# Reciprocals of linear attention spread to the heads' rows by DMA instead of by matmul

## What is computed

```python
qp = _phi(proj(Wq, bq))          # elu(x) + 1
kp = _phi(proj(Wk, bk))
v = proj(Wv, bv)
def step(carry, inp):
    kv, ksum = carry
    kt, vt, qt = inp
    kv = kv + jnp.einsum('bhd,bhe->bhde', kt, vt)
    ksum = ksum + kt
    num = jnp.einsum('bhd,bhde->bhe', qt, kv)
    den = jnp.einsum('bhd,bhd->bh', qt, ksum)[..., None] + EPS
    return ((kv, ksum), num / den)
```

## Time and profile before

| | us |
|---|---|
| median of three runs | 1916.9 (1913.78 to 1916.97) |
| profiled execution | 1916.06 |
| its span | 1914.3 |
| PE busy | 1890.7 |
| DVE busy | 1569.2 |
| POOL busy | 889.8 |
| ACT busy | 663.8 |

### The profile page before, as it was taken

How to read it: one execution, slowest core, us unless ns; L and a number is a source line. 1 busy time by engine, 2 the same in 40 slices (tenths; PEclk the granted TensorE clock), 3 DMA queues, 4 the chain that set the end, 5 groups by cost and what they waited for, 6 DMA issues and landing times.

```text
span 1914.3 us, 60181 instructions
## 1 busy us (share of the span) xinstructions
PE 1890.7 (99%) x25412; PEld 1659.6 (87%) x25412; DVE 1569.2 (82%) x3356; ACT 663.8 (35%) x1298; POOL 889.8 (46%) x981
## 2 busy tenths in 40 slices
PE   7999999999999999999999999999999999999997
PEld 6888888888888888888888888888888888888887
DVE  7888787888879888778878888887888897888888
ACT  4333333323333332333333433333333333323331
POOL 4345554455443554534554445544345553455422
PEclk9999999999999999999999999999999999999999
DMA  6343234333243432343323334333443234333222
GB/s 215 101 128 112 96 106 128 118 118 112 90 127 119 127 121 74 123 125 116 123 89 118 117 112 136 100 98 113 128 128 112 85 114 130 117 117 113 89 73 90
DMA packets 171197, 217.97 MB, mean 114 GB/s; under 512 B 24368, under 2 KB 85808, under 8 KB 170928
## 3 DMA queue, kind: packets, MB, share of 16 engines
q1 hardware_dynamic: 170928, 214.13, 35.4%
HBM read 151.02 MB, written 63.04 MB: 112 GB/s over the span
## 4 chain that ended last, share of the span: by engine, by line
PE 95%; DVE 2%; POOL 1%; DMA 1%; issue 0%; SPq 0%; ACT 0%; POOLq 0%; DVEq 0%
PE ring L684 38%; PE ring L666 36%; PE ring L758 7%; PE num_ps L788 6%; PE num_ps L771 3%; PE num_ps L801 2%; PE ring L730 1%; PE ring L743 1%; DMA v_tok<-in_wv_t 1%; DVE s_mask L973 0%; PE ring L654 0%; DVE stats L1091 0%; DVE den L1220 0%; DVE res L1084 0%; DVE o_lo L1215 0%
## 5 line engine op out<-in xcount | busy, mean ns | idle before, releaser
L1315 POOL TENSOR_TENSOR k_sum<-k_sum,q_raw 128x512 f32<-128x512 f32 x128 | 165.3, 1291 | 545.0 <-DVE q_raw L984 545.0
L883 ACT ACTIVATE e_tmp<-ring,bias_n 128x512 f32<-128x512 f32 x256 | 175.9, 687 | 509.3 <-PE ring L666 508.7
L973 DVE TENSOR_TENSOR s_mask<-ring,causal 128x512 f32<-128x512 f32 x512 | 315.0, 677 | 0.0
L684 PE MATMUL ring<-wv_hi,xt_hi 128*128 128x260 f32 x1024 | 298.9, 292 | 0.0
L684 PE MATMUL ring<-wv_hi,xt_lo 128*128 128x260 f32 x1024 | 289.2, 282 | 0.0
L684 PE MATMUL ring<-wv_lo,xt_hi 128*128 128x260 f32 x1024 | 289.2, 282 | 0.0
L684 PE MATMUL ring<-wo_hi,o_hi 128*128 128x260 f32 x1016 | 284.8, 281 | 1.3 <-ACT o_hi L938 1.3
L684 PE MATMUL ring<-wo_lo,o_hi 128*128 128x260 f32 x1016 | 285.7, 282 | 0.0
L684 PE MATMUL ring<-wo_hi,o_lo 128*128 128x260 f32 x1016 | 285.5, 284 | 0.2 <-DVE o_lo L1215 0.2
L938 ACT ACTIVATE o_hi<-num_ps 128x512 fp32r<-128x512 f32 x127 | 75.8, 597 | 465.9 <-PE num_ps L788 465.9
L666 PE MATMUL ring<-xt_hi,wk_hi 128*128 128x512 f32 x512 | 207.2, 405 | 3.4 <-DVE xt_lo L1042 1.7
(11 more groups left out here) (147 smaller groups left out, 3955.4 us busy)
## 6 DMA issues: line engine op xcount, KB each, us to landing
x_tok<-in_x SPq DMA_DIRECT2D x128, 256.0 KB, 3.8
res<-in_x SPq DMA_DIRECT2D x128, 256.0 KB, 2.8
out<-res SPq DMA_DIRECT2D x128, 256.0 KB, 2.1
x_in<-in_x_t SPq DMA_DIRECT2D x124, 256.0 KB, 4.7
keys_turned<-k_turned SPq DMA_DIRECT2D x112, 256.0 KB, 2.0
k_tok<-keys_turned SPq DMA_DIRECT2D x448, 64.0 KB, 2.1
x_rows<-moments_rows SPq DMA_DIRECT2D x31, 512.0 KB, 3.6
k_t<-in_wk_t SPq DMA_DIRECT2D x4, 256.0 KB, 4.5
```

Of the source, the lines that this page charges most:

```text
L684: mm = pe.matmul(bank[:, 0:HW], rows[a](k), w[b][:, k, h, :], start=n == 0, stop=n == 3 * KD - 1)
L883: act.activation(e_tmp[:, m], bank, ACT.Relu, bias=bias_n[:, m, g:g + 1], scale=-1.0).then_inc(phi_relu.handle, 1)
L973: dve.tensor_tensor(s_mask[:, j], ring[:, st.bank(u)].rearrange("p (g t) -> p g t", g=KD), repeat(causal, KD), ALU.mult).then_inc(free[st. ...
L1315: pool.tensor_tensor(k_sum[:, g], k_sum[:, g], q_raw[:, g], ALU.mult).then_inc(prod.handle, 1)
```

## The change

The eight products with `spread` are gone, and with them the high and low parts (`rden_high`, `rden`, `lo_rows`, `spread`), the bank uses ("R", g) and ACT's copy. The denominators are summed in another form: `head_cols` now has four sets of columns, one for each tile of 128 tokens, and the result is 128 partitions by 128 columns (16 products of 128 columns, going round the four groups). They stand ahead of `from_tile` now, "in front of the values" that are summed by the masked scores. DVE inverts 128 columns. SP stores the reciprocals (64 KB) to a DRAM tensor `den_rows`; when they have landed, SP (heads 0 and 1) and ACT (heads 2 and 3) issue eight DMAs of 128 KB that read them back, each value to the 32 rows of its head, into `k_sum`, whose products are no longer needed. In the first block SP issues all eight. DVE then divides from `k_sum` and `q_raw`, both in SBUF, in two instructions of 128x1024, one for each half of the block's tokens, with the values between them. The ring has 42 uses instead of 48. The moments of tile 2's residual (`residual_moments`) stay directly behind the residual; before, they came after the divisions. The scratch of the expert choice has a buffer of its own.

```diff
-SKIPS = {0: 1, 3: 2}
+SKIPS = {3: 1}
...
-        uses += [("O", (c, 0)), ("O", (c, 1))] + [("R", g) for g in range(KD)] * (c == 2)
+        uses += [("O", (c, 0)), ("O", (c, 1))]
...
+    def spread_reciprocals(eng, b, heads):
+
+        eng.wait_ge(den_out.handle, 16 * (b + 1))
+        for half in range(2):
+            t = slice(half * BT // 2, (half + 1) * BT // 2)
+            for j in heads:
+                pieces = slice((2 * j + half) * TPB // 2, (2 * j + half + 1) * TPB // 2)
+                rows = den_dram[:, pieces, :].rearrange("g s t -> g (s t)").unsqueeze(0)
+                eng.dma_start(k_sum[j * HD:(j + 1) * HD, :, t], rows.to_broadcast([HD, KD, BT // 2])
+                              ).then_inc(den_in[half].handle, 16)
...
+        def send_reciprocals(b):
+            sp.wait_ge(den_rec.handle, b + 1)
+            sp.dma_start(den_dram.rearrange("g r t -> (g r) t"), den).then_inc(den_out.handle, 16)
...
                 if c == 2:
                     send_keys(t, 3)
+                    if st.has("proj"):
+                        send_reciprocals(t + 1)
+                        spread_reciprocals(sp, t + 1, (0, 1))
                     fetch_keys(t, 3)
...
-            for g in range(KD):
-                for s in range(2):
-                    mm = pe.matmul(bank[g * HD:(g + 1) * HD, 0:BT // 2], head_cols[:, s],
-                                   k_sum[:, g, s * BT // 2:(s + 1) * BT // 2], start=s == 0, stop=s == 1,
-                                   tile_position=(0, g * HD))
+            for s in range(TPB):
+                for g in range(KD):
+                    mm = pe.matmul(bank[g * HD:(g + 1) * HD, 0:P], head_cols[:, s],
+                                   k_sum[:, g, s * P:(s + 1) * P], start=s == 0, stop=s == TPB - 1,
+                                   skip_group_check=True, tile_position=(0, g * HD))
...
+            if c % 2 == 0:
+                pe.wait_ge(divided.handle, 2 * off + c // 2 + 1)
...
                     add_state(st, c)
+                    if c == 2 and proj:
+                        denominators(st)
                     from_tile(st, c)
...
-                if c == 2 and attn and proj:
-                    spread_reciprocals(st)
...
                 if attn:
                     keep_state(st, c)
...
+                if c == 2 and attn and proj:
+                    spread_reciprocals(act, st.off + 1, (2, 3))
...
-        def divide(st):
-
-            for g in range(KD):
-                u = ("R", g)
-                dve.wait_ge(full[st.bank(u)].handle, st.filled(u))
-                bank = ring[:, st.bank(u)]
-                dve.tensor_tensor(q_div[:, (st.off + 1) % 2, g], bank, q_raw[:, g], ALU.mult).then_inc(free[st.bank(u)].handle, 1)
+        def invert(st):
+
+            dve.wait_ge(free[BANK[("DEN", 0)]].handle, st.freed(("DEN", 0)))
+            dve.reciprocal(den, den).then_inc(den_rec.handle, 1)
+
+        def divide(st, half):
+
+            dve.wait_ge(den_in[half].handle, 16 * HPG * (st.off + 2))
+            t = slice(half * BT // 2, (half + 1) * BT // 2)
+            dve.tensor_tensor(q_div[:, (st.off + 1) % 2, :, t], k_sum[:, :, t], q_raw[:, :, t], ALU.mult
+                              ).then_inc(divided.handle, 1)
...
                 if last and proj and attn:
-                    divide(st)
-                if last and attn and proj:
-                    residual_moments(st, 2)
+                    divide(st, 0)
                 if proj:
                     chunks(st, c, 0, 1)
-                if last and not attn:
-                    divide(st)
+                if last and proj and attn:
+                    divide(st, 1)
```

More of the change, by code:

```diff
@@ L416, in set_constants @@
         link(pool.memset(head_cols, 0.0))
-        for s in range(2):
-            for h in range(2):
-                row = 2 * HPG * s + HPG * h
-                link(pool.tensor_copy(head_cols[:, s, row:row + HPG], head_of_row))
+        for s in range(TPB):
+            rows = head_cols[:, s, 0:HPG * TPB].rearrange("p (j s) -> p j s", j=HPG)
+            link(pool.tensor_copy(rows[:, :, s], head_of_row))
         link(pool.memset(kv_diag, 0.0))
-        link(pool.memset(row_of_group, 0.0))
-        for g in range(KD):
-            link(pool.affine_select(out=row_of_group, in_=row_of_group, compare_op=ALU.not_equal, fill=1.0,
-                                    base=-g * HD, pattern=[[-1, 2 * 2 * HPG]], channel_multiplier=1))
         for e in range(E):
@@ L443, in attention @@
     k_scan, k_carried, prod = sem("k_scan"), sem("k_carried"), sem("prod")
-    den_rec, rden_hi, rden_parts = sem("den_rec"), sem("rden_hi"), sem("rden_parts")
+    den_rec, den_out, den_in, divided = sem("den_rec"), sem("den_out"), [sem(f"den_in{n}") for n in range(2)], sem("divided")
     summed, lower_summed = sem("summed"), sem("lower_summed")
@@ L602, in body @@
                 send_keys(t + 1, 0)
+                send_reciprocals(t + 1)
+                spread_reciprocals(sp, t + 1, range(HPG))
                 fetch_keys(t + 1, 0)
@@ L832, in body @@
                     sum_columns(pe)
-                if c == 2 and proj:
                     denominators(st)
@@ L930, in body @@
                     exponential(act, 4)
+                if c == 2 and proj:
+                    u = ("DEN", 0)
+                    act.wait_ge(full[st.bank(u)].handle, st.filled(u))
+                    act.activation(den, ring[:, st.bank(u), 0:P], ACT.Copy, bias=DEN_EPS
+                                   ).then_inc(free[st.bank(u)].handle, 1)
                 if st.alone() and last:
@@ L938, in body @@
                     act.activation(o_wide[0], num, ACT.Copy).then_inc(o_hi.handle, 1)
-                if c == 2 and proj:
-                    u = ("DEN", 0)
-                    act.wait_ge(full[st.bank(u)].handle, st.filled(u))
-                    for m in part_begun(st.off - 1):
-                        act.wait_ge(chosen.handle, (m + 1) * CHOOSE_STEPS)
-                    act.activation(den, ring[:, st.bank(u), 0:BT // 2], ACT.Copy,
-                                   bias=DEN_EPS).then_inc(free[st.bank(u)].handle, 1)
                 if attn:
                     keep_state(st, c)
-                if c == 2 and proj:
-                    act.wait_ge(den_rec.handle, den_rec.at(st.lin(1, st.off + 1, 1)))
-                    act.activation(rden_high, den, ACT.Copy).then_inc(rden_hi.handle, 1)
+                if c == 2 and attn and proj:
+                    spread_reciprocals(act, st.off + 1, (2, 3))
                 if proj:
@@ L1201, in body @@
                     split_x_low(st, 1)
+                if last and not attn:
+                    divide(st, 0)
                 if c == 2 and attn:
@@ L1207, in body @@
                     turn_keys(st.off, 2)
+                if c == 2 and proj:
+                    invert(st)
                 if st.alone() and last:
@@ L1217, in body @@
                     sum_state(st, c)
-                if c == 2 and proj:
-                    dve.wait_ge(free[BANK[("DEN", 0)]].handle, st.freed(("DEN", 0)))
-                    dve.reciprocal(den, den).then_inc(den_rec.handle, 1)
                 if not last and attn:
@@ L1253, in body @@
                     residual(st, c)
[L1254 to L1255 removed]
+                    residual_moments(st, c)
                 if c == 0 and proj:
@@ L1271, in set_first @@
                 split_low(dve, name, g)
-            set_from_constants(dve)
+            for name in BY_COLUMNS:
+                dve.wait_ge(ready[name].handle, KD)
+            dve.wait_ge(const_set.handle, CONSTS)
             dve.wait_ge(row_load.handle, ROWS)
```

52 lines of the change are left out of this document (9 added, 43 removed).

## The result

| | before | after |
|---|---|---|
| median of the runs | 1915.34 us (1913.59 to 1916.97, 4 runs) | 1961.51 us (1953.95 to 1961.94, 4 runs) |
| profiled execution | 1916.1 us, span 1914.3 us | 1953.95 us, span 1952.2 us |
| ratio after / before | 1 | 1.0232, 95% interval 1.0215 to 1.0250 |

The change makes the kernel 2.3% slower. The forecast was 1954 us: the profiled execution is there, the three others, at 1961.3 to 1961.9, are 7.5 us above it.

What follows compares the result with a forecast made beforehand. PE bounds the kernel (busy 1890.7 of 1914.3 us), and longer DVE work now delays it. Ordinary blocks +28.1, late blocks +6.7, start +3.5, last block -0.6 make +37.7 on 1916.1: 1954 us, range 1922 to 1976.

Steps and rivals of the forecast that it cites:

- Spread matmuls, -0.63 us a block: On PE between output tile 2 and the next values: dropping the spread saves 0.63 us a block, 19.5 us in all.
- Denominators, 0: On PE: the new form takes 0.88 us for the same 2048 columns, a change of 0 (-0.2 to +0.1).
- The way of the reciprocals, costed at nothing: Store to DRAM and read back before DVE's divisions: rows land on time with little to spare, cost nothing.
- k_tok lands a microsecond or more before PE wants them: Even blocks, SP's queue: k_tok DMAs leave at about 925, not 922.3, land near 929, still early enough; no cost.
- Collisions, +1.55 us: DVE's two divisions wait for POOL's SBUF instructions, so xt_lo starts 1.55 us later (1.3 to 1.8).
- late blocks: Four of 30 blocks with POOL 0.7 us later: DVE's stretch grows 2.05 us, PE loses 1.68 us each.
- The wait of 0.15 us from DVE to PE: Before the next block's first K product: about 0.15 us from DVE's end to PE's start, when PE waits.
- The sum: Whole run: ordinary blocks 28.1, late blocks 6.7, start +3.5, last block -0.6, together +37.7 us.
- Start, +3.5 us: Block 0, once: the first K product waits for the masked scores' bank under the 42-use ring, +3.5 us.
- from below +2.7: Lower bound of the start delay: block 0's first K product waits until the masks are over, taken as 60.65.
- K0 waiting 1 us some 30 times, as the longest wait: Expected profile sign: PE's first K product of a block waits about 1 us for xt_lo, some 30 times.
- waits for k_tok as a sign of being wrong: Stated refutation: the prediction is wrong if PE waits for k_tok or at the scores instead of for xt_lo.

Runs made afterwards that it cites:

- the last kernel: Changed kernel with division 0 behind tile 2's values, division 1 later, half 1's rows, add_state and GpSimd's bias add delayed, ring of 48 uses: 1907.20 us, ratio 0.9954.
- k_tok first: Changed kernel with tile 3's k_tok fetches on SyncE's queue issued between half 0's and half 1's spreading DMAs: 1963.19 us, ratio 1.0241.
- the first experiment: Kernel before the change, its four divisions multiplying by a constant in SBUF in place of the spread rows in PSUM: 2002.79 us, ratio 1.0447.

## Why the prediction was right

- **Spread matmuls, -0.63 us a block: held.** In the last kernel undisturbed blocks are 58.56 and 57.89 us apart in place of 59.19 and 58.27; with the 0.20 us wait in odd blocks taken off, PE is 0.60 us a block shorter.
- **Denominators, 0: held.** In the changed kernel they take 219.78 - 218.91 = 0.87 us from start to start (0.88 in the earlier trace rows), 1.10 us busy in both forms and both orders over the tiles. From K0 to the next T0 the last kernel takes 46.59 and 45.98 us, the kernel before 46.60 and 45.98.
- **The way of the reciprocals, costed at nothing: held here, not in itself.** The rows of before that I used (2.1 us for 64 KB, 3.6 us for the broadcast) were too short: the spreading lands after 4.2 us in the median (2.6 to 7.0). Even so half 0 was there at T0 + 1.0 in the median (I had + 0.2 to + 1.5), and division 0 waited for it once, 0.4 us. "k_tok lands a microsecond or more before PE wants them" is the step that failed. Its DMAs leave at T0 - 1.9 in the median, as I had it (- 1.8), but one takes 4.7 us in place of 2.0, so that the last lands at T0 + 4.4 and not + 2.2. PE asks at T0 + 3.75 and waited in 12 of 15 blocks. It cost nothing here because VectorE's stretch was longer: in ten of the twelve K0 waited for xt_lo after all, and the other two are no longer than their like. With that stretch gone it cost 14.8 us.
- **Collisions, +1.55 us: held in mechanism and nearly in size.** xt_lo begins 1.42 us later in the median, with both divisions behind POOL's work in the order written down. GpSimd comes late (its last normalise begins after T0 + 2.0) in seven blocks, not four. In three of them division 0 got in ahead of the normalise (1.3 us), the xt_lo pair met the bias add, and K0 is late by 1.2 to 1.3 us; in two the order is the one forecast for late blocks, and K0 is late by 1.6 and 1.7 us (forecast 1.68); the last two follow below.
- **The wait of 0.15 us from DVE to PE: too large.** K0 starts 0.05 us behind the end of the last xt_lo. In the blocks from 168.30 and 227.66 us K0 is 0.94 (odd) and 0.83 us (even) late, where the prediction had 1.13 and 1.03.
- **What made up for it.** The sum had (28.1 + 6.7) / 30 = 1.16 us a block, the profile has 1.17, but by other terms: 23 ordinary blocks 19.6 us; the five late ones 7.0; two blocks (T0 = 886.16 and 947.53), where x_rows landed some 1.7 us later than usual, 3.1 and 2.2 us, the first with the clock at half for a stretch, the second with k_tok late too; 4.4 us between K0 and the next T0 (46.72 us from 241.08 on, for 46.60), mostly in the first product of K0, which stands at 0.50 for 0.39 us in its record; and -0.9 us, since in two blocks of before L1231 met GpSimd and held up the spreading by 0.4 us. The last three were not in the sum; that they nearly make up for the smaller ordinary delay is luck.
- **Start, +3.5 us: +4.0 at the first T0, but not by the path given.** K0 starts at 60.26, 2.2 us late, below my "from below +2.7": I had put the end of the masks at 60.65, the start of the next work on DVE. The other 1.8 us are the granted clock at half behind that wait, for which the sum had nothing. In seven traces of kernels with the same ring the first K0 starts at 61.3 to 63.6 us, so the profiled run of the change has the shortest start of all.
- **Signs.** "K0 waiting 1 us some 30 times, as the longest wait" was only half right: 26 waits of up to 0.6 us. The rest of the delay stands as waits for s_mask and k_tok just ahead of it in the same stretch, which are no separate losses, but for the 2.0 us for s_mask that the half clock followed. I had named waits for k_tok as a sign of being wrong; they are none where they lie under a wait of the same stretch.
- **Luck in the number.** Three of four runs of the change took 1961.5 us and the profiled one 1953.95, so the forecast of 1954 meets the fastest run and is 7.5 us under the median. No slower run of this kernel was traced, but its neighbours were: with k_tok first (profiled 1963.64 us) and with the denominators behind from_tile (1963.86 us) the first T0 lies at 110.9 and 112.1 us (108.2 here), and the 30 periods take 1804.0 and 1803.4 us (1798.0 here). Both have one more stretch at half clock ahead of the first step, and in the blocks one and two of them, each behind a wait of 2.0 to 2.4 us for s_mask or k_tok; those three blocks are 1.9 to 2.1 us longer than the median. A longer start and more blocks with late landings are therefore the likely place of the 7.5 us; for the change itself that is not shown. A wait of 2.04 us for k_tok at 951.3 us in the change was followed by no such stretch, nor one of 2.8 us in the run with the halved divisions, so what decides it stays open too.

## What to carry to other kernels

Before an operand of a VectorE instruction moves from PSUM to SBUF, look at what GpSimd does at that moment: if both then read SBUF, each waits for the whole instruction of the other, and the price is read from the neighbours' end times. Where they must meet, make the VectorE side few and long instructions, put its PSUM work beside GpSimd's, and hold GpSimd's work back until then. And a wait that costs nothing today should be priced as if its cover were gone, since the next edit will take the cover away. Behind the longest waits of TensorE, read its granted clock as well: here a stretch at half clock cost 1.7 us or more beside the wait.

## What the runs showed of the hardware

- Taking turns by the instruction: four divisions of 0.68 us each became 1.76 us in the median, two of 1.2 us became 2.3 and 1.5 us, and halving the two put xt_lo off by another 1.0 us in the median. In the first experiment I had reckoned with one or two waits for the four, and got three.
- The exclusion costs GpSimd as much as VectorE: its bias add went from 1.29 to 2.28 us in the record, though nothing waited for it.
- A broadcast of 1 KB rows of a DRAM tensor to 32 partitions, 128 KB, takes 4.2 us to land in the median and 0.43 us to issue, up to 1.48 us at worst on SyncE's queue. With eight such DMAs about, the 64 KB fetches of k_tok take 4.7 us to land in the median in place of 2.0.
- TensorE's granted clock fell from 2.4 to 1.2 GHz behind some waits of 1.8 to 4.4 us, in the middle of a kernel that keeps it 97% busy: products of 512 columns then start 0.43 us apart in place of 0.23, and a stretch of 3.4 us cost about 1.7 us. In the kernel before, whose longest wait between the first block and the last is 1.3 us, it never fell there.
